# Feed-forward stage of a fused attention and expert block: where the last group's hidden values, its norms, turns and the first query products stand

## The reference, cut to what matters

```
x = layer_norm(x + attn, g1, b1)
gate = x @ Wg + bg
up = x @ Wu + bu
ffn = (silu(gate) * up) @ Wd + bd
y = layer_norm(x + ffn, g2, b2)
x = x_in + y
...
q = x @ Wq.T            # 16 heads of 16, softmax attention with a mask over keys
```

## Time and profile before

| | us |
|---|---|
| median of 3 runs | 1027.9 |
| lowest and highest run | 1027.07 and 1030.37 |
| profiled execution, its own time | 1029.43 |
| span of that execution in the trace | 1027.7 |
| PE busy in it | 886.8 (86%) |
| DVE busy | 747.3 (73%) |
| POOL busy | 425.7 (41%) |
| ACT busy | 394.8 (38%) |

### The profile page before, as it was taken

The page is one execution under the profiler, slowest core; times in us unless marked ns, Lnnn a source line. Parts: engine busy times, 40 slices in busy tenths (PEclk is TensorE's granted clock), DMA queues, the critical chain, the costliest instruction groups (busy, mean ns, idle before and its releaser), DMA issues. The chain is left out here.

```text
span 1027.7 us, 17852 instructions
## 1 busy us (share of the span) xinstructions
PE 886.8 (86%) x5607; PEld 756.1 (74%) x5616; DVE 747.3 (73%) x1449; ACT 394.8 (38%) x746; POOL 425.7 (41%) x489
## 2 busy tenths in 40 slices
PE   4399999999937676799988689988899999999998
PEld 1399999999936565587777655536688888888887
DVE  5888888888826878767876766628677777767676
ACT  4356666666414332413344245568511111111110
POOL 3177777777720224275533722220133333333332
PEclk9599999999978888899989899999999999999999
DMA  8336213135143000050003920000000100101002
GB/s 267 110 98 201 96 41 123 41 124 175 41 126 124 1 0 1 12 186 1 1 1 60 192 68 1 1 1 27 6 17 15 31 21 25 29 17 31 15 0 82
DMA packets 50300, 61.80 MB, mean 60 GB/s; under 512 B 8015, under 2 KB 37769, under 8 KB 50249
## 3 DMA queue, kind: packets, MB, share of 16 engines
q1 hardware_dynamic: 43464, 43.85, 13.9%
q0 software_dynamic: 6336, 17.31, 7.0%
q10 hardware_dynamic: 448, 0.01, 0.0%
HBM read 47.26 MB, written 7.60 MB: 53 GB/s over the span
## 5 line engine op out<-in xcount | busy, mean ns | idle before, releaser
L2145 POOL TENSOR_TENSOR kTh<-at_acc,kTh 128x512 fp32r<-128x512 f32 x68 | 88.2, 1297 | 257.1 <-DVE kTh L2323 257.1
L2071 ACT ACTIVATE at_acc<-psum 128x512 f32<-128x512 f32 x68 | 40.8, 601 | 240.0 <-PE psum L1873 240.0
L2405 DVE SCALAR_TENSOR_TENSOR y<-psum,at_pT,y 128x256 f32<-128x256 f32 x272 | 112.3, 476 | 0.1
L1915 PE MATMUL psum<-at_wkh,kTh 128*128 128x256 f32 x544 | 107.7, 282 | 3.0 <-DVE y L2405 3.0
L1873 PE MATMUL psum<-act_hi,at_wkh 128*128 128x512 f32 x272 | 108.5, 399 | 0.3 <-ACT at_acc L2071 0.3
L1873 PE MATMUL psum<-act_hi,at_wkl 128*128 128x512 f32 x272 | 107.6, 396 | 0.0
L1873 PE MATMUL psum<-act_lo,at_wkh 128*128 128x512 f32 x272 | 107.5, 395 | 0.0
L2320 DVE TENSOR_TENSOR at_acc<-psum,at_acc 128x512 f32<-128x512 f32 x68 | 47.0, 692 | 74.3 <-PE psum L1873 60.9
L444 ACT ACTIVATE e_u<-psum,e_bias 128x256 f32<-128x256 f32 x152 | 63.8, 472 | 95.9 <-PE psum L343 86.9
L1915 PEld LDWEIGHTS psum<-at_wkh,kTh 128*128 128x128 f32 x544 | 88.8, 190 | 7.0 <-DVE y L2405 3.0
L1915 PE MATMUL psum<-at_wkl,kTh 128*128 128x256 f32 x272 | 76.5, 281 | 0.0
(11 more groups left out here) (498 smaller groups left out, 2839.5 us busy)
## 6 DMA issues: line engine op xcount, KB each, us to landing
e_raw<-in_W SPq DMA_DIRECT2D x16, 512.0 KB, 6.9
e_raw<-in_W SPq DMA_DIRECT2D x8, 1024.0 KB
y<-in_x SPq DMA_DIRECT2D x4, 512.0 KB, 9.5
v_tok<-in_xT SPq DMA_DIRECT2D x4, 512.0 KB, 8.1
y<-y_rows SPq DMA_DIRECT2D x4, 512.0 KB, 7.4
v_tok<-y_rows SPq DMA_DIRECT2D x4, 512.0 KB, 8.4
v_tok<-in_x SPq DMA_DIRECT2D x4, 512.0 KB, 8.9
e_raw<-in_w_gate SPq DMA_DIRECT2D x16, 128.0 KB, 2.1
```

The source lines that it names most:

```text
L1915: last = pe.matmul(ps[4 + j][:, 0:D], hh[a][:, s % HS, j * P:(j + 1) * P], e2_w[par][b][:, OD:OD + D], start=n == 0, stop=n == 2)
L2071: act.activation(sl_sb[:, s % 2, :], ps[s % 2][:, :], ACT.Silu).then_inc(esil, 1)
L2145: pool.tensor_tensor(hh[1][:, s % HS, :], h32[:, s % 2, :], hh[0][:, s % HS, :], ALU.subtract).then_inc(hsp, 1)
L2405: dve.scalar_tensor_tensor(out=y[:, i, :], in0=ps[4 + j][:, 0:D], scalar=comb[:, i, bass.ds(2 * t + out_s // G, 1)], in1=y[:, i, :], op0=A ...
```

## The change

In six parts:

1. **Bias adds on POOL** (`if m % 2 and s < 4 * G`): the eight adds stand behind steps s = 1, 3, 5, ..., 15 in the order y, v_tok, y, v_tok, and so on; before they stood behind the chunks m = 1 and m = 3 of every group, which is s = 1, 3, 7, 9, 13, 15, 19, 21. The last group has none.
2. **Mask counts on DVE** (`COUNTED`): all eight in groups 1 and 2, at m = 0, 2, 3, 5; before three in each of groups 1 and 2, at m = 2, 3, 5, and two in group 3.
3. **Last two low halves on DVE** (`low_part`): steps 22 and 23 are split by DVE itself; `hidden(23)` waits for `hsp` 23 instead of 22.
4. **`gain(2)`** stands behind `hidden(23)` (m = 5), before behind `hidden(22)` (m = 4).
5. **`turn(2)`** stands inside `down(3)`, behind its second tile, before ahead of `down(3)`; `hi(2)` on ACT stands behind the second square root, `lo(2)` on DVE behind `norm_last(1)`.
6. **Query products**: u = 0 and 1 ahead of `down(3)`, u = 2 and 3 behind it and ahead of `turn_last`; before 0 to 2 between `down(3)` and `turn_last`, and 3 at the end.

```
-                COUNTED = (2, 3, 5)
+                COUNTED = {g * FC + m: (g - 1) * 4 + n for g in (1, 2) for n, m in enumerate((0, 2, 3, 5))}
...
+                def low_part(eng, s):
+                    eng.wait_ge(hhi, s + 1)
+                    eng.tensor_tensor(hh[1][:, s % HS, :], h32[:, s % 2, :], hh[0][:, s % HS, :], ALU.subtract).then_inc(hsp, 1)
...
                             last.then_inc(ops, 1)
+                            if g == L1 and j == 1:
+                                turn(g - 1)
...
-                        else:
-                            turn(g - 1)
-                            down(g)
                     pe.wait_ge(qsplit, 2)
-                    for u in range(QE - 1):
+                    for u in range(2):
+                        pe.wait_ge(h32d, NS - 1 + u)
+                        query_product(pe, wq, u, qps)
+                    down(L1)
+                    for u in range(2, QE):
                         query_product(pe, wq, u, qps)
                     turn_last()
-                    query_product(pe, wq, QE - 1, qps)
...
-                    hi(L1 - 1)
                     for i in range(L1 * TG, NT):
+                        if i == L1 * TG + 2:
+                            hi(L1 - 1)
...
+                        if s < NS - 2:
+                            low_part(pool, s)
...
-                        if m in (1, 3):
-                            sl = slice(g * TG, (g + 1) * TG)
-                            if m == 1:
+                        if m % 2 and s < 4 * G:
+                            r = s // 2 // 2
+                            sl = slice(r * TG, (r + 1) * TG)
+                            if s // 2 % 2 == 0:
...
                         if s >= 2:
-                            dve.wait_ge(hsp, s - 1)
+                            dve.wait_ge(hsp, s if s == NS - 1 else s - 1)
...
+                        if s >= NS - 2:
+                            low_part(dve, s)
...
-                        if g and m == 4:
+                        if g and m == (FC - 1 if g == L1 else 4):
                             gain(g - 1)
-                        if g and m in COUNTED and (g - 1) * 3 + COUNTED.index(m) < QT:
-                            count((g - 1) * 3 + COUNTED.index(m))
-                    lo(L1 - 1)
+                        if s in COUNTED:
+                            count(COUNTED[s])
...
                         norm_last(j)
+                        if j == 1:
+                            lo(L1 - 1)
```

More of the change, by code:

```diff
@@ L1229, in stage_feed_forward @@
                 NS = G * FC
-                COUNTED = (2, 3, 5)
+                COUNTED = {g * FC + m: (g - 1) * 4 + n for g in (1, 2) for n, m in enumerate((0, 2, 3, 5))}
+                assert len(COUNTED) == QT
                 QE = 2 * KC
@@ L1359, in _ @@
                         g, m = s // FC, s % FC
-                        pool.wait_ge(hhi, s + 1)
-                        pool.tensor_tensor(hh[1][:, s % HS, :], h32[:, s % 2, :], hh[0][:, s % HS, :],
-                                           ALU.subtract).then_inc(hsp, 1)
+                        if s < NS - 2:
+                            low_part(pool, s)
                         if g == 2 and m == 0:
@@ L1372, in _ @@
                             else:
-                                pool.wait_ge(xin[g], 16)
+                                pool.wait_ge(xin[r], 16)
                                 pool.tensor_tensor(xk[:, sl, :], xk[:, sl, :], group_rows(gb[:, 1, :]), ALU.add).then_inc(xbiased, 1)
```

## The result

| | before | changed |
|---|---|---|
| median, 17 runs each (us) | 1028.38 | 1022.84 |
| lowest and highest run | 1027.07 and 1030.37 | 1020.79 and 1028.13 |
| profiled execution, its own time | 1029.43 | 1021.08 |
| span in the trace | 1027.7 | 1018.9 |

The ratio is 0.9947 (95%: 0.9934 to 0.9959): the change saves 5.5 us, 0.53%. The forecast was 4.3 us.

A forecast was written before the change was run, and what follows sets the result against it. The bound was PE's pause before the last product, paid again as slow low-clock matmuls. Gains of 6.0 us net of the head's 1.0, less 1.7 at the opening, gave 4.3: 1027.9 to 1023.6 us, range 1020.6 to 1027.2.

The forecast's parts named there:

- The stage's end: Feed-forward stage's end: last product gains 2.9 us; then gains of 1.9, 0.6 and 1.9, less 1.3 for `lo(2)`.
- cover of 0.6: Last group on DVE: `gain(2)` ends 0.6 us before the first sum is due, so it costs nothing.
- The head: Groups 0 to 2 of the feed-forward stage: moving adds and counts costs 1.0 us, bounds 0 and 2.0.
- whatever pauses these bring stay: Steps 9 and 15 still have an add behind them, so their pauses were taken as unchanged.
- the add behind step 11: New POOL add holds the CAST of step 12 and delays the sums of `down(1)`: cost 1.0 us.
- Rival F: PE still pauses before the last product; each us costs one, above 3 us the clock falls; chance 0.02.
- Two counts saved win nothing: Group 3: PE was never idle in its four `up` steps, so dropping two DVE counts there gains nothing.
- The opening: Start of the attention stage: a PE pause of 4.4 us brings a clock fall, costing 1.7 us (1.2 to 2.7, or zero).
- Rival B: The clock holds at the opening of attention, so the whole 6.0 us is gained: 1021.9 us; chance 0.20.
- D: Gain given back by a later DVE chain, late mask or costlier low clock; 0 to 3 us remain, about 1026.5; chance 0.16.
- E: Slower: the low clock stays through the attention scores, up to 12 us more, all of it 1035.6; chance 0.05.
- C: The CAST behind step 11 costs nothing, no pause in `down(1)`: adds 1.0 us of gain, 1022.6; chance 0.09.

The follow-up runs named there:

- e3: The changed kernel with part 6 alone undone, query products in their old places: 1025.12 us, ratio 0.9965 to the kernel before.
- e6: The changed kernel with part 3 alone undone, low halves of steps 22 and 23 back on POOL: 1025.7 us, ratio 0.9955 to the kernel before.
- e7: The changed kernel with part 4 alone undone, `gain(2)` ahead of step 23 again: 1025.11 us, ratio 0.9952 to the kernel before.
- e8: The changed kernel with part 5 alone undone, `turn(2)`, `hi(2)`, `lo(2)` ahead of the last product: 1025.05 us, ratio 0.996 to the kernel before.
- e1: The kernel before with parts 1 and 2 alone, bias adds and mask counts moved: 1029.19 us, ratio 1.000.
- e9: e5 with fifteen idle matmuls filling PE's pause into the attention stage: 1016.65 us, ratio 0.9887 to the kernel before.
- e5: The changed kernel with six of the bias adds behind steps 7 and 13, during `down(0)` and `down(1)`: 1015.97 us, ratio 0.9862 to the kernel before.
- e2: The changed kernel with parts 1 and 2 undone, so parts 3 to 6 only: 1023.98 us, ratio 0.9952 to the kernel before.
- e11: The changed kernel run again unchanged, on the chip of e9 and e10: 1021.35 us, ratio 0.9934 to the kernel before.
- e10: The kernel before with the changed kernel's counts and the adds of e5, without parts 3 to 6: 1018.31 us, ratio 0.9901.
- e4: The changed kernel with query product 3 alone put back behind `turn_last`: 1022.0 us, ratio 0.994 to the kernel before.

## Why the prediction was right, and where not

- **The stage's end, 37.57 to 30.6 forecast: 30.32 measured.** Every step of it was found in the trace: no pause ahead of the last product, first sum 2.45 behind it (2.42), DVE's end 545.65 as against 546.5, `hi(3)` 0.43 behind it (0.4), no wait of `lo(2)`. The points of time lie 0.7 to 0.9 before those forecast, mostly because the stage began 2.0 earlier in this trace and its head took 1.4 more than forecast. e3, e6, e7 and e8 show that parts 3 to 6 each carry weight, and e6 that the low halves had to leave POOL for a reason that the prediction didn't have.
- **`gain(2)`, cover of 0.6:** it ended 0.66 ahead of the first sum. Right.
- **The head, cost 1.0 forecast: 2.4 in the trace.** The step that failed is "whatever pauses these bring stay". The term for the add behind step 11 was right in mechanism (CAST 2.20) and too large (0.68). But a pause of 2.15 was taken as a fixed cost, and it isn't: it brings a fall of the clock of 1.55 us or it doesn't. The pauses stay, the falls behind them are the rest. Rival F's reading, that a pause brings a fall above 3 us (an estimate between the 2.81 without one and the 4.18 with one), fell with it: falls followed pauses of 2.13 to 2.18 us. Against a typical execution of before the head probably costs less than 2.4 (above, argued).
- **"Two counts saved win nothing":** nothing in the rows speaks against it; no run moved the counts alone. e1's gain in B is that of the hole, where the add stood beside the CAST.
- **The opening, cost 1.7 forecast: 0.64 at the last scores.** Pause (4.4 forecast, 4.17), fall, and DVE's wait (about 3, 2.92) came as told, and the key product was 1.29 late. The step that failed is the one after: that all of this delay reaches the end. Half of the 1.29 us was given back, first in the key products, where the kernel before had its own fall; e9, which removes fall and delay, is 0.5 ahead of e5 at the last scores and has no gain in its median. The prediction asked what is late next and stopped too early. Its own bounds were loose: 2.5 for 1.4 us makes 1.1 and not 1.2 at least (1.05 measured in DVE's wait), and 2.7 at most has no working behind it. Its other bound, zero, was met in no trace: all seven with the pause of 4.17 have the fall (PEclk 0.50 to 0.60 in the 4 us behind the pause).
- **The sum:** forecast -6.0 + 1.7 = -4.3; measured -5.5. By the traces it is -7.25 + 2.4 = -4.9 up to the attention stage, and -4.2 at the last scores. That this is nearly the forecast is luck: the two misses, 1.4 too little in the head and 1.1 too much in the opening, nearly cancel. What makes the median fall by 1.3 us more than that isn't shown. Rival B's 6.0 us is nearer to the measured 5.5 than the forecast, for the wrong reason: the clock did not hold. Rivals D and E have no support; F and C are refuted by the rows.

## What to carry to other kernels

A bulk operation on GpSimd that reads on-chip memory is placed by what VectorE does beside it: behind the steps where VectorE only drains PSUM it held nothing here (sums of 0.42 us beside it and without it, e5), beside a cast it holds the cast (2.20 us instead of 0.43; here 5.6 us of the stage with the fall that it brought, about as much as the whole change). A pause of TensorE of about 2 us inside dense work is to be closed even when its own length seems cheap, since it may be paid a second time as a fall of the clock (1.55 us here). Independent products that must be made anyway are a good filler, and taking them away from where others wait behind them can be worth more than the clock that they keep (e3: 1.6 us against 0.8). When a fall of the clock is costed, follow it to the next place where the work meets the transfers or a fall of its own; of a delay that is only moved there, little is left.

## What the hardware showed beyond expectation

- A fall of the clock behind a pause of 2.15 us (PEclk 0.59 to 0.67 in the 4 us behind it, in the changed kernel, e2 and e11): in nine of ten traces at step 17 and in four of ten at step 13, though the pauses have the same length to 0.04 us. A pause of 2.81 us at the border of the stages had none right behind it in the kernel before, e1 and e10, and one within about 1 us in e3 and e4 (PEclk 0.63 and 0.56 in the 4 us behind it, against 1.00). Pauses of 0.4 had none in three kernels (e5, e9, e10).
- One such fall cost 1.55 us (13.08 against 11.52, the same in three traces to 0.01).
- GpSimd is held by VectorE as well as the other way: a low half took 2.17 to 2.28 instead of 1.27 to 1.29 when a pass of `gain` had begun 0.08 to 0.16 earlier, and the next pass of `gain` then took 2.17 to 2.20 instead of 1.21.
- A reduction of 128x1024 bytes on VectorE was not held: 1.21 us beside GpSimd and (but for 0.06 us) without it.
